# Routing of tokens to experts: ranks counted across a panel's three tiles on TensorE, probabilities placed ahead of the ranks

## The reference, cut to what matters

```python
gate_scores = jnp.einsum('bsd,ed->bse', x, Wg) + bg
topk_scores, topk_idx = jax.lax.top_k(gate_scores, K)          # K = 2 of E = 8
topk_probs = jax.nn.softmax(topk_scores, axis=-1)
combine = jnp.sum(topk_probs[..., None] * jax.nn.one_hot(topk_idx, E, dtype=x.dtype), axis=-2)
for e in range(E):
    h = jax.nn.relu(jnp.einsum('bsd,hd->bsh', x, W1[e]) + b1[e])
    y = jnp.einsum('bsh,dh->bsd', h, W2[e]) + b2[e]
    out = out + combine[..., e:e + 1] * y
```

## Time and profile before

| | |
|---|---|
| median of three runs | 1946.84 us (1945.93 to 1947.46) |
| the profiled execution, its own time | 1950.9 us |
| its span | 1949.1 us |
| mean granted TensorE clock | 0.965 of full speed |
| TensorE matmul busy | 1807.9 us, 93% of the span, 12680 instructions |
| TensorE weight load busy | 1702.0 us, 87%, 12680 instructions |
| VectorE busy | 1616.5 us, 83%, 4226 instructions |
| ScalarE busy | 1331.3 us, 68%, 2651 instructions |
| GpSimd busy | 959.1 us, 49%, 1703 instructions |

### The profile page before, as it was taken

The page is one execution under the profiler, slowest core; times in us unless marked ns, Lnnn a source line. Parts: engine busy times, 40 slices in busy tenths (PEclk is TensorE's granted clock), DMA queues, the critical chain, the costliest instruction groups (busy, mean ns, idle before and its releaser), DMA issues. The chain is left out here.

```text
span 1949.1 us, 41788 instructions
## 1 busy us (share of the span) xinstructions
PE 1807.9 (93%) x12680; PEld 1702.0 (87%) x12680; DVE 1616.5 (83%) x4226; ACT 1331.3 (68%) x2651; POOL 959.1 (49%) x1703
## 2 busy tenths in 40 slices
PE   6799999829999999858999979999999999999997
PEld 4689999829999999857888869999999999999997
DVE  5689878739999999738656559999999999999996
ACT  4434555416666666543555459999999999999995
POOL 2000134535555555530101027777777777777774
PEclk8889999959999999979999999999999999999999
DMA  8676778237887887543556400000000000000002
GB/s 310 207 250 201 218 200 179 96 136 215 233 234 232 236 237 228 133 170 104 193 173 203 143 17 2 2 2 2 2 1 2 2 2 2 2 2 2 2 2 71
DMA packets 97235, 226.26 MB, mean 116 GB/s; under 512 B 20897, under 2 KB 51363, under 8 KB 88620
## 3 DMA queue, kind: packets, MB, share of 16 engines
q1 hardware_dynamic: 82476, 206.33, 33.8%
q0 software_dynamic: 14592, 17.91, 4.7%
HBM read 204.43 MB, written 19.75 MB: 115 GB/s over the span
## 5 line engine op out<-in xcount | busy, mean ns | idle before, releaser
L2028 PE MATMUL ffn_psH<-ffn_w2h,ffn_vTh 128*128 128x256 f32 x1320 | 393.0, 298 | 1.5 <-DVE ffn_u L2084 1.5
L2028 PE MATMUL ffn_psH<-ffn_w2h,ffn_vTl 128*128 128x256 f32 x1320 | 374.3, 284 | 0.0
L2028 PE MATMUL ffn_psH<-ffn_w2l,ffn_vTh 128*128 128x256 f32 x1320 | 373.9, 283 | 0.0
L2117 POOL TENSOR_SCALAR ffn_vn<-ffn_vn,ffn_rstd,ffn_shift 128x256 f32<-128x256 f32 x540 | 300.0, 560 | 21.1 <-issue 1.2
L2072 DVE BATCH_NORM_STATS2 ffn_stats<-ffn_vn 128x6 f32<-128x256 f32 x780 | 284.5, 406 | 25.0 <-ACT ffn_vn L2054 23.9
L2084 DVE SCALAR_TENSOR_TENSOR ffn_u<-ffn_th,ffn_psH 128x512 f32<-128x512 f32 x390 | 263.5, 676 | 7.4 <-ACT ffn_th L2051 7.4
L2028 PEld LDWEIGHTS ffn_psH<-ffn_w2h,ffn_vTh 128*128 128x128 f32 x1320 | 253.0, 192 | 2.5 <-DVE ffn_u L2084 1.7
L2028 PEld LDWEIGHTS ffn_psH<-ffn_w2l,ffn_vTh 128*128 128x128 f32 x1320 | 253.2, 192 | 0.8
L2028 PEld LDWEIGHTS ffn_psH<-ffn_w2h,ffn_vTl 128*128 128x128 f32 x1320 | 252.5, 191 | 0.0
L2054 ACT ACTIVATE ffn_vn<-ffn_u 128x512 f32<-128x512 f32 x390 | 248.7, 638 | 0.8 <-DVE ffn_u L2084 0.8
L2051 ACT ACTIVATE ffn_th<-ffn_psH 128x512 f32<-128x512 f32 x390 | 232.6, 596 | 1.7 <-PE ffn_psH L1991 1.7
(11 more groups left out here) (240 smaller groups left out, 5021.6 us busy)
## 6 DMA issues: line engine op xcount, KB each, us to landing
g_raw<-in_adjt SPq DMA_DIRECT2D x168, 384.0 KB, 4.8
g_raw<-in_wide SPq DMA_DIRECT2D x78, 512.0 KB, 3.7
moe_w1raw<-in_wall SPq DMA_DIRECT2D x33, 1024.0 KB, 5.2
moe_w2raw<-in_wall SPq DMA_DIRECT2D x33, 1024.0 KB, 5.9
moe_b<-in_eb SPq DMA_DIRECT2D x33, 128.0 KB, 4.5
g_raw<-in_adjl SPq DMA_DIRECT2D x14, 256.0 KB, 2.8
g_raw<-in_narrow SPq DMA_DIRECT2D x13, 256.0 KB, 2.6
xn_rows<-rt_hn SPq DMA_DIRECT2D x8, 384.0 KB, 4.2
```

The lines of the kernel that those rows point to most:

```text
L2028: last = pe.matmul(psH[w % R][:, q * D:(q + 1) * D], a[:, w % R, q * KD + k, :], b[:, k, :], start=(k == 0 and j == 0), stop=(k == KD - 1 ...
L2117: last = pool.tensor_scalar(vn[:, t, :], vn[:, t, :], rstd[:, s:s + 1], shift[:, s:s + 1], ALU.mult, ALU.add)
```

## The change

`rank` now works out ranks across the whole panel on TensorE. The matmul with `before` stays, as the start of an accumulation; for each tile but the last, a matmul with `ones` adds that tile's counts to the columns of all later tiles (the counts are read through a broadcast view); and one matmul with `ones` per tile accumulates the panel's total into eight columns. For three tiles that is six matmuls in place of two, for two tiles four.

On VectorE, `count` becomes one addition (ranks plus the free slots at the panel's start, for all tiles at once, by a broadcast view); it takes over the addition that `give_slots` began with. The copy and the additions tile by tile go away. A new step `keep_free`, behind `give_slots`, adds the panel's total to the free slots, which now alternate between two buffers, and signals a new semaphore `freed`, for which VectorE itself waits too. `weigh` moves from turn +26 to +25 and `count` from +25 to +26. `gate` of the next panel waits for `freed` in place of `slots_done`.

```diff
-        self.free = sb("rt_free", [P, PT + 1, E])
+        self.free = sb("rt_free", [P, 2, E])
...
+        freed = sem("freed")
...
-                dve.tensor_copy(route.free[:, PT, :], route.reg_i[:])
+                dve.tensor_copy(route.free[:, 0, :], route.reg_i[:])
...
             def count(k):
                 n = len(tiles_of(ORDER[k]))
-                had = len(tiles_of(ORDER[k - 1])) if k else PT
                 free = route.free
                 dve.wait_ge(rank_done, k + 1)
-                chain(dve.tensor_copy(free[:, 0, :], free[:, had, :]))
-                for t in range(n):
-                    chain(dve.tensor_tensor(free[:, t + 1, :], free[:, t, :],
-                                            psR[:, (2 * PT + t) * E:(2 * PT + t + 1) * E], ALU.add))
+                bc = [P, n, E]
+                chain(dve.tensor_tensor(pos[:, 0:n, :], psR[:, PT * E:(PT + n) * E].rearrange("p (t e) -> p t e", e=E),
+                                        free[:, k % 2, :].unsqueeze(1).broadcast_to(bc), ALU.add))
...
             def give_slots(k):
                 n = len(tiles_of(ORDER[k]))
-                chain(dve.tensor_tensor(pos[:, 0:n, :], route.free[:, 0:n, :],
-                                        psR[:, PT * E:(PT + n) * E].rearrange("p (t e) -> p t e", e=E), ALU.add))
                 for r in range(2):
...
+            def keep_free(k):
+                at = 2 * PT * E
+                dve.tensor_tensor(route.free[:, (k + 1) % 2, :], route.free[:, k % 2, :], psR[:, at:at + E],
+                                  ALU.add).then_inc(freed, 1)
+                dve.wait_ge(freed, k + 1)
...
-                done = len(tiles_of(ORDER[-1]))
-                chain(dve.tensor_tensor(count[:], route.free[:, done, :], route.reg[:], ALU.subtract))
+                chain(dve.tensor_tensor(count[:], route.free[:, GROUPS % 2, :], route.reg[:], ALU.subtract))
...
                 if place_at(m, 25) is not None:
-                    count(place_at(m, 25))
+                    weigh(place_at(m, 25))
                 if place_at(m, 26) is not None:
-                    weigh(place_at(m, 26))
+                    count(place_at(m, 26))
                 if place_at(m, 27) is not None:
                     give_slots(place_at(m, 27))
+                    keep_free(place_at(m, 27))
...
                 if k == 0:
                     pe.wait_ge(placed, 64)
                 else:
-                    pe.wait_ge(slots_done, k)
+                    pe.wait_ge(freed, k)
...
-                pe.matmul(psR[:, PT * E:(PT + n) * E], g.before[:], flat, start=True, stop=True)
-                pe.matmul(psR[:, 2 * PT * E:(2 * PT + n) * E], g.ones[:], flat, start=True, stop=True).then_inc(rank_done, 1)
+                pe.matmul(psR[:, PT * E:(PT + n) * E], g.before[:], flat, start=True, stop=False)
+                for t in range(n - 1):
+                    pe.matmul(psR[:, (PT + t + 1) * E:(PT + n) * E], g.ones[:],
+                              chosen[:, t:t + 1, :].broadcast_to([P, n - 1 - t, E]), start=False, stop=(t == n - 2))
+                for t in range(n):
+                    last = pe.matmul(psR[:, 2 * PT * E:(2 * PT + 1) * E], g.ones[:], chosen[:, t, :], start=(t == 0),
+                                     stop=(t == n - 1))
+                last.then_inc(rank_done, 1)
```

## The result

The changed kernel takes **1952.05 us** in the median of 16 runs, the kernel before 1947.03 us in 16 runs beside it: the ratio is 1.0027, with a 95% interval from 1.0021 to 1.0034, so the change costs about 5.0 us (4.1 to 6.6). Forecast were 1951.4 us and +4.6 us. The profiled execution took 1954.7 us with a span of 1952.6 us; that of before 1950.9 and 1949.1 us.

The account below looks back on a forecast made before the run. TensorE was taken to bound the second sweep, a chain of small steps the tail. The terms 5.4 - 0.83 + 0 + 0.0 = +4.6 us, on the 1946.84 us median, gave 1951.4 us; 8-in-10 range 1946.9 to 1953.4.

Parts of the forecast that it names:

- VectorE's relief is worth nothing in the sweep: Second sweep: VectorE loses about 0.6 us of work per panel, but nothing waits for it, so 0 gained.
- The price of a pass: Ranks in the sweep: each extra narrow fp32 pass costs 0.104 us, between 0.0975 and 0.11, read from the gate.
- The term of 5.4 us: Second sweep: seven ranks get 52 more TensorE passes at 0.104 us, costing 5.4 us (5.1 to 5.7).
- The wait at k = 3: Sweep, TensorE's 1.07 us wait ahead of `turn_normed`: hides the longer rank of k = 2, -0.83 us (0 to -1.07).
- those rows depend on work that lies ahead of the rank of k = 2: Sweep: ScalarE's normalised rows for k = 3 do not depend on that rank, so its extra 0.83 us falls into the wait.
- The sum: Whole kernel: 5.4 - 0.83 + 0 + 0.0 = +4.6 us, 1951.4 us on the median; chance 0.68.
- The tail: Last panel, behind the sweep: longer rank and shorter VectorE chain cancel, 0.0 us; from half a microsecond lost to 1.4 gained.
- Repeated weights cost nothing: Rival, ranks: five matmuls with the same `ones` need one load; sum about -1.1 us, 1945.7 us; chance 0.10.
- issue gap of some 25 ns: Sweep: the skill's figure for a narrow matmul alone would make 52 passes 1.3 us; gate rows spoke against it.
- The clock stays up: Rival, tail: TensorE's clock holds at 1.00 to the last rank, -2.6 us, so +2.0 in sum, 1948.8 us; chance 0.14.
- VectorE late: Rival, sweep: `count` waits 0.83 us in seven panels, delaying low parts; 5.8 us more, about 1957 us; chance 0.04.
- spare time of 1.3 us: Sweep, VectorE: `count` of k = 6 started 1.3 us behind its rank's end, taken as margin against the longer rank.

Follow-up runs that it names:

- e1: The kernel before with only as many extra ones passes behind every rank as the change adds, into unread PSUM columns: 1951.98 us, ratio 1.0036.
- e2: The kernel before with the extra ones passes only for k = 0 to 6, in the sweep but not the tail: 1953.41 us, ratio 1.0033.
- e4: The changed kernel with its ranks in fp32r, one pass per matmul, so 6 passes in place of 12 for three tiles: 1946.80 us, ratio 1.0006.
- e12: The changed kernel with `turn_normed` one turn later (+10 in place of +9): 1952.20 us, ratio 1.0027 to the kernel before.
- e3: The kernel before with only `weigh` moved ahead of `count`, no extra pass: 1945.73 us, ratio 0.9998.
- e7: The kernel before with only `turn_normed` one turn later (+10 in place of +9): 1944.07 us, ratio 0.9989.
- e5: The changed kernel with tiles summed on VectorE right behind `choose`, two matmuls (4 passes) a rank, rank one turn later: 1948.31 us, ratio 1.0012.
- e6: As e5, with the ranks in fp32r besides, two passes a panel: 1946.45 us, ratio 1.0001 to the kernel before.
- e8: As e6, with `turn_normed` one turn later (+10 in place of +9): 1943.40 us, ratio 0.9988 to the kernel before.
- e11: The kernel before with `weigh` ahead of `count` and `turn_normed` one turn later: 1945.48 us, ratio 0.9995.
- e9: As e6, with the sums in a step of their own one turn later, behind `aggregate`, and the rank one turn later: 1944.06 us, ratio 0.9988.

## Why the prediction was right, and where its numbers were off

**The mechanism held.** The change pays for VectorE's steps with TensorE's passes, and in the sweep TensorE is the engine that waits only once, at k = 3. e1 and e2 show that the passes alone give the loss; e4, which takes 40 of the 52 away, takes most of it back; e12 shows them bare. That VectorE's relief is worth nothing in the sweep holds too: without the waits the sweep of after is 144.8 us, and those of e1 and e2, which have the passes and none of the relief, are 144.9 and 144.7. e3 shows that the new order alone leaves the sweep where it was.

**The price of a pass** was taken as 0.104 us from the gate, between 0.0975 and 0.11. Measured: 0.1056 from the sweeps of e12 and e7, 0.112 from the ranks alone. The term of 5.4 us is 5.5 by the sweep and 5.8 by the ranks, just above the bound of 5.7. The gate was the right row: twelve passes with a load each, at the same clock.

**The wait at k = 3** is the term that was mis-sized: -0.83 us was forecast, -0.43 measured in the profiled execution. The step that failed is "those rows depend on work that lies ahead of the rank of k = 2". Their inputs do lie ahead, but the change also moves what VectorE does beside GpSimd's steps in between: a low part now runs beside the last of them, and that step took 0.60 us in place of 0.19. e1 and e4 show the two parts: the longer rank alone fills 0.85 us of the wait, as forecast, and VectorE's changed steps alone make the wait about 0.4 us longer. That it is the low part that holds GpSimd's step is read from rows. The wait itself is not in every execution (e2 and e3 had none, with the same `turn_normed`), which the prediction's bound of zero allowed for.

**The sum** with both terms as measured is 5.5 - 0.4 = 5.1 us; the marks give 5.16, the medians 1952.05 - 1947.03 = 5.0. That the medians come so near is in part luck: their interval is 4.1 to 6.6 us, and they hold executions with and without the wait in shares that no run shows.

**The tail** came out as forecast to 0.01 us: count 2.77 us behind the rank's start, as the gate at the same clock had it, and 3.21 us from `chosen` to the product as before. It is a balance: +1.69 us of passes (e1) against -0.89 for the order (e3) and -0.80 for the copy and the additions.

**The rivals.** *Repeated weights cost nothing*: out by the 40 loads for 20 matmuls and by e1's 0.21 us a pass at the lower clock, six and eight in a row. The price does not follow the columns, as it is 0.112 us for 16 and for 8 alike. That it is the price of the weight load is argued, as no run has a pass without one. The Trainium skill (TensorE: Matmul & The Clock Gate, section LDWEIGHTS) gives a load as columns / 1.2 in ns, for 128 columns an estimated 107 ns. The rows at full clock agree (104 to 112 ns a pass), those at the lower clock take twice that. Something like the issue gap of some 25 ns that the prediction weighed shows only behind a first pass whose load ran beside the contraction ahead of it. In before that is the rank of k = 0 (PE timeline), whose first two passes take 0.14 us where those of k = 6 take 0.25:

```profile
262.01 0.30 PE L973 MATMUL g_psR<-rt_chosen,before 128*128 128x24 f32 x2
262.15 0.38 PE L974 MATMUL g_psR<-rt_chosen,ones 128*128 128x24 f32 x2
```

*The clock stays up*: the rank of k = 7 runs at the upper level in the profiled execution of after (its twelve passes are busy for 1.50 us, those of k = 8 for 2.73), and the granted clock of the stretch is 0.55 in place of 0.50, but the gate of k = 8 starts at 393.55 and VectorE follows at 396.38, 2.83 us later, as slow as before. *VectorE late*: it did not happen with the change, as the one wait of TensorE shows. But the reason that I gave, spare time of 1.3 us, is a margin of one place on VectorE, ahead of `count`; e5 and e6 show that some turns earlier, between `choose` and `aggregate`, the margin is below half a microsecond.

## What to carry to other kernels

Before work is moved from one engine to another, ask for each stretch which of the two has the waits: here four freed steps of VectorE were worth 0.80 us in the one panel whose chain is bare, and the passes that replaced them cost 5.5 us in the seven panels where TensorE is full. Count a matmul of a few columns by its passes and weight loads, not by its columns, and price it from a row that has the same passes in a row. Where an engine seems to have slack, look at the place, not at the sum: with the same three instructions ahead of `aggregate` TensorE waited 4.8 us in six panels, and with them one turn later 2.0 us in two.

## What was not expected of the hardware

GpSimd's first step, one instruction on 128 x 3 elements, takes 0.19 to 0.41 us in most panels and 1.96 us at k = 3, to the hundredth, in before, after, e1, e4, e5, e6, e7, e8, e11 and e12. VectorE's timeline of before around it, of which the first and the last steps stand here:

```profile
297.95 0.55 DVE L611 TENSOR_TENSOR g_lo<-g_raw,g_hi 128x384 fp32r<-128x384 f32 x1
298.42 0.28 DVE L618 TENSOR_TENSOR g_raw<-g_raw,ident 128x128 f32<-128x128 f32 x1
...
299.29 0.55 DVE L611 TENSOR_TENSOR g_lo<-g_raw,g_hi 128x384 fp32r<-128x384 f32 x1
299.76 0.18 DVE L693 COPY rt_free<-rt_free 128x8 f32<-128x8 f32 x1
```

From 297.95 to 299.84 VectorE runs five instructions on two tensors from SBUF without a pause (three low parts and two additions of the identity), and GpSimd's step, begun at 297.95, ends at 299.91, 0.07 us behind the last of them. In e3, with the same VectorE steps, it gets in behind the first:

```profile
296.25 0.55 DVE L611 TENSOR_TENSOR g_lo<-g_raw,g_hi 128x384 fp32r<-128x384 f32 x1
...
296.24 0.61 POOL L847 TENSOR_SCALAR g_veps<-g_mv 128x3 f32<-128x3 f32 x1 [2.85 <-DVE g_mv L652]
```

It ends at 296.85, 0.05 us behind the end of that low part, and TensorE has no wait. e1 and e2, which are the same program up to the rank of k = 7, differ in the same way: 1.96 and 0.61 us. e9's 1.50 us at k = 2 end at 276.23, behind three low parts that end at 276.16. The Trainium skill (SBUF — State Buffer, section Who interferes with whom) says that a VectorE instruction with two inputs in SBUF contends with a GpSimd instruction that reads SBUF, and calls the ports that they share an exclusive lock. The rows agree, and show in addition that the step may be held by five such instructions in a row or by one, from one profiled execution to another. With `turn_normed` at +9, TensorE had a wait at k = 3 in every profile with the 1.96 us and none in the two with 0.61. What decides between them stays open.
